# A selective scan: the input increments of every unit's last tile move from VectorE to GpSimd, and that tile's decay from SBUF to PSUM

## The chip, the cores and the metric

The kernel runs on one core of a Trainium2 chip. The metric is the device time of one execution in microseconds (us); lower is better. The engines named below are TensorE (PE in the rows), VectorE (DVE), ScalarE (ACT), GpSimd (POOL) and SyncE (SP), which here only issues DMAs. Each runs its own instruction stream in order, and they wait for each other on semaphores.

## The reference

The program is a convolution-like state-space layer followed by attention and a mixture of experts. The change lies in the first part, a selective scan over images of 4 x 192 channels x 32 x 32, so over L = 1024 positions. There are four directions k: row by row, column by column, and both reversed.

```python
x_dbl = jnp.einsum('bkdl,kcd->bkcl', xs, x_proj_weight)
dts, Bs, Cs = (x_dbl[:, :, :R], x_dbl[:, :, R:R + N], x_dbl[:, :, R + N:])
dt = jax.nn.softplus(dts + bias)
def step(h, inp):
    dtt, ut, bt, ct = inp
    dA = jnp.exp(dtt[..., None] * A)
    h = h * dA + (dtt * ut)[..., None] * bt[:, :, None, :]
    y = jnp.einsum('bkdn,bkn->bkd', h, ct)
    return (h, y)
...
ys = ys + Ds * u;  y = cross_merge(ys);  y = layernorm(y);  out = gelu(y)
```

For each of 192 channels d and 16 states n a first-order recurrence h = h * decay + increment runs over the 1024 positions. The decay is exp(dt * A), the increment is dt * u * B. Each state is then multiplied by C and the 16 are summed.

## The kernel before

**Tiles and units.** A unit is one image b, one direction k and one half f of the channels (96 of them). There are `UNITS = 8` for each image, in the order given by `order(ui)`: p (row order or column order), f, r (forward or reversed). The outer loop `Fori(0, NB, 1)` runs over the four images, so there are 32 units. A unit has `TILES = 12` tiles. A tile holds 32 channels times 4 states on 128 partitions and all 1024 positions: tile t has channel block j = t % 3 and state group nq = t // 3. Each tile is worked in two halves of 512 positions, numbered q = 2t and 2t + 1 in a unit, 24 of them.

**What happens to a half tile q.** TensorE spreads the 4 B rows over the 128 partitions with a selection matrix, into one of the `UR = 4` PSUM banks of `psU` (L426); it waits until scan q - 4 is done, because that one read the bank. VectorE multiplies the bank in place with `dtu_rep`, dt*u replicated to 128 partitions by DMA (L610, called the product below). ScalarE makes the decay of a whole tile in SBUF, `decay` (L519), up to four tiles ahead. VectorE then runs the scan (L655): it reads the decay (SBUF) and the increment (PSUM) and writes `hs`, a ring of 8 tiles in SBUF. The second half of a tile starts from the last state of the first and waits for it.

**After the scan.** GpSimd multiplies the finished tile with the replicated C rows, `c_rep` (L565). TensorE adds up the states of three tiles at a time, one "trip" of 2 x 3 f32 matmuls, into `psY` (L395, `sum_states`). Over two units, forward and reversed, `psY` collects one result. ScalarE copies it to `y_new` (L499, `read_y`, at tile 7 of the next even unit), and GpSimd adds it to `Y` (L547, L550, `add_y`, at tile 6).

**What is prepared for the next unit.** During tiles 0 and 1 of every unit TensorE projects dt of the next one (L359, `z_side`), ScalarE takes it out and makes the softplus, and GpSimd finishes dt after tile 3 (L570) and dt*u after tile 4 (L576). SyncE stores both in DRAM and loads them back replicated (L664), four slots each. In units 2 and 6 TensorE also projects the B and C rows of the next row order or column order at tiles 4 and 5 (L359 again, `row_side`), and GpSimd works on them after tile 8 of that unit and after tile 6 of the next (L582, L591).

**Order of the work.** Nothing is scheduled automatically: each engine's stream is written out in the loops. VectorE issues the product of q + 1 before the scan of q; TensorE issues at position q the spread of q, then the projection, then the trip, if one stands there.

Of the kernel before, what the change touches and what calls it, by code (L numbers as in the profile page):

```python
# [25 lines left out]
NB = 4  # L26
D = 192
HC = 96
# [42 lines left out]
def prepare(nc, w, s):  # L71

    with ExitStack() as ctx:
# [30 lines left out]
        with nc.Block() as block:  # L104
# [36 lines left out]
            def _(pool):  # L141
# [46 lines left out]
                pool.memset(s.X[:, NB, :, :], 0.0)  # L188
# [85 lines left out]
def scan(nc, w, s):  # L274

    with ExitStack() as ctx:
# [6 lines left out]
        HR, DR, UR, RR = 8, 4, 4, 4  # L283
        xt = sb("xt", [HC, 2, L])
# [9 lines left out]
        y_new = sb("y_new", [HC, L])  # L294
# [25 lines left out]
        y_begun = sem("y_begun")  # L320

# [7 lines left out]
        def source(nb, p):  # L329
            return (lambda h, lo, n=CH: xt[:, h, lo:lo + n]) if p else (lambda h, lo, n=CH: s.X[:, nb, h, lo:lo + n])  # L330

        def unit_ahead(b, ui):

            return b + (ui + 1) // UNITS, (ui + 1) % UNITS

        def row_step(b, ui):

            return (b, 1, b * 2 + 1) if ui < 4 else (b + 1, 0, b * 2 + 2)
# [11 lines left out]
        with nc.Block() as block:  # L350
            @block.tensor
            def _(pe):
# [10 lines left out]
                def z_side(q, b, ui):  # L363
# [6 lines left out]
                    if q == 0:  # L370
                        pe.wait_ge(row_taken, b * 4 + (2 if ui < 3 else 4 if ui < 7 else 6))
                        if p:
                            pe.wait_ge(xt_half, nb * 2 + 2)
                    project(psP[0:HC, c, :], s.w_dt[:, k, h, HC * f:HC * f + HC], source(nb, p)(h, CH * c), h, z_proj)

                def row_side(q, b, ui, n):
# [5 lines left out]
                    if q == 8:  # L382
                        pe.wait_ge(z_taken, n * 2 + 4)
                        if p:
                            pe.wait_ge(xt_half, nb * 2 + 2)
# [26 lines left out]
                with pe.Fori(0, NB, 1) as b:  # L412
                    for ui in range(UNITS):
# [29 lines left out]
            def _(act):  # L443
# [48 lines left out]
                def read_y(n, pair, b, ui):  # L492
# [5 lines left out]
                    act.wait_ge(y_added, pair + (1 + START))  # L498
                    nc.scalar.copy(y_new[:], psY[0:HC, :, :].rearrange("p c l -> p (c l)")).then_inc(y_taken, 1)  # L499
# [9 lines left out]
                with act.Fori(0, NB, 1) as b:  # L509
                    for ui in range(UNITS):  # L510
                        n = b * UNITS + ui
                        p, f, r, k = order(ui)
                        for t in range(TILES):
# [4 lines left out]
                            act.wait_ge(scan_done, n * (2 * TILES) + (2 * t + 2 - 2 * DR + S0))  # L518
                            nc.scalar.activation(decay[:, t % DR, :], dt_rep[:, rep_slot(ui, j), :], ACT.Exp,  # L519
# [5 lines left out]
                            if ui == UNITS - 1 and t in (5, 6):  # L525
# [3 lines left out]
                                               s.X[:, b + 1, h, :].rearrange("p (h w) -> p w h", h=HH)  # L529
# [4 lines left out]
            def _(pool):  # L534
                pool.sem_inc(y_added, 1 + START)

# [1385 lines left out]
```

## Time and profile before

| | |
|---|---|
| time, median of 3 runs | 2926.32 us (2926.2 to 2936.25) |
| the profiled execution's own time | 2925.74 us |
| its span | 2923.9 us |
| scan loop, first product to last scan | 66.6 us to 1424.5 us |
| VectorE busy in the whole span | 2180.1 us (75%) |
| GpSimd busy in the whole span | 1266.4 us (43%) |

The scan takes a little under half of the time; attention and the experts follow it and are not touched. How the rows below are read: in a timeline row the first number is the start in us from the span's start, the second how long the group of x instructions took from the first start to the last end, and the square bracket tells how long the engine had sat idle before and what ended that. Neighbouring instructions of one engine overlap a little, so the time that one takes out of the stream is the distance from its start to the next one's start, which is less than its duration.

### The profile page before, as it was taken

The numbers are of one execution on the slowest core, as the hardware profiler recorded it, in microseconds if no ns is written. First come the engines' busy times: TensorE is split into PE (matmuls) and PEld (weight loads), VectorE is DVE, ScalarE is ACT, GpSimd is POOL, SyncE is SP. The second block draws the span as 40 slices with busy tenths as digits, with TensorE's granted clock in tenths as the row PEclk, the third lists the DMA queues.
The fourth block names the chain that finished last, engine by engine and source line by source line (L and its number), as shares of the span: only waits on it lengthen the run. The fifth ranks groups of instructions, "written<-read, shape, count | busy, mean of one in ns | idle before, by whom it ended". The sixth has DMA issues, their size and how long they took to land. (4 is left out here: it accounts for less than half of the span.)

```text
span 2923.9 us, 33177 instructions
## 1 busy us (share of the span) xinstructions
PE 2319.4 (79%) x8931; PEld 816.1 (28%) x8931; DVE 2180.1 (75%) x3002; ACT 1349.9 (46%) x1866; POOL 1266.4 (43%) x651
## 2 busy tenths in 40 slices
PE   3676767667676766667668599999999969999999
PEld 1111111111111111111124122333333227676766
DVE  4999999999999999999656598787878642221212
ACT  3454454445444443544456067676767532222221
POOL 3888887888788788888731200000000020000000
PEclk9777676767777677777669599999999979999999
DMA  4434443443454344345413512131221340000000
GB/s 121 157 118 149 160 135 124 164 158 121 137 162 145 120 156 158 118 139 165 128 34 93 80 16 30 25 45 24 35 33 24 46 126 6 6 6 6 6 6 11
DMA packets 92071, 255.58 MB, mean 87 GB/s; under 512 B 16430, under 2 KB 22129, under 8 KB 91857
## 3 DMA queue, kind: packets, MB, share of 16 engines
q1 hardware_dynamic: 87818, 253.41, 31.1%
q8 instruction: 66, 1.08, 0.2%
q10 hardware_dynamic: 4078, 0.19, 0.1%
q14 instruction: 109, 0.89, 0.1%
HBM read 209.25 MB, written 40.04 MB: 85 GB/s over the span
## 5 line engine op out<-in xcount | busy, mean ns | idle before, releaser
L565 POOL TENSOR_TENSOR hs<-hs,c_rep 128x1024 f32<-128x1024 f32 x384 | 901.0, 2356 | 258.7 <-DVE hs L655 225.1
L426 PE MATMUL psU<-b_stack,b_sel 96*128 96x512 bf16 x768 | 370.4, 492 | 429.9 <-DVE hs L655 428.0
L519 ACT ACTIVATE decay<-dt_rep,a_neg 128x1024 f32<-128x1024 f32 x384 | 437.2, 1145 | 484.1 <-DVE hs L655 470.9
L1529 DVE TENSOR_REDUCE mx<-ps 128x1 f32<-128x512 f32 x864 | 539.3, 682 | 114.7 <-PE ps L1368 109.5
L1504 ACT ACTIVATE P<-ps 128x512 f32<-128x512 f32 x768 | 417.6, 599 | 246.3 <-PE ps L1380 222.0
L610 DVE TENSOR_TENSOR psU<-psU,dtu_rep 128x512 f32<-128x512 f32 x768 | 513.8, 673 | 23.4 <-PE psU L426 13.1
L655 DVE TENSOR_TENSOR_SCAN hs<-decay,hs,psU 128x512 f32<-128x512 f32 x384 | 487.4, 1269 | 1.1
L655 DVE TENSOR_TENSOR_SCAN hs<-decay,psU 128x512 f32<-128x512 f32 x384 | 463.5, 1207 | 0.0
L395 PE MATMUL psY<-hs,state_sel 128*32 128x512 f32 x1572 | 421.4, 895 | 21.5 <-ACT y_new L499 15.4
L1368 PE MATMUL ps<-ks,qs 96*128 96x512 bf16 x864 | 344.2, 403 | 34.6 <-DMA ks<-qk_parts 24.2
L426 PEld LDWEIGHTS psU<-b_stack,b_sel 96*128 96x128 bf16 x768 | 75.9, 100 | 993.0 <-DVE hs L655 869.3
L1817 DVE SCALAR_TENSOR_TENSOR acc<-psE,gate,acc 128x192 f32<-128x192 f32 x128 | 53.5, 418 | 381.9 <-PE psE L1717 378.9
L1380 PE MATMUL ps<-qs,ks 99*128 99x512 bf16 x768 | 293.4, 382 | 0.0
L1755 ACT ACTIVATE hid<-psH,b 128x512 f32<-128x512 f32 x192 | 114.6, 695 | 317.6 <-PE psH L1709 317.6
L1717 PE MATMUL psE<-w,hid 128*128 128x192 f32 x1536 | 257.1, 328 | 0.0
L1717 PEld LDWEIGHTS psE<-w,hid 128*128 128x128 f32 x1536 | 248.8, 190 | 21.2 <-ACT hid L1755 21.2
L1393 PE MATMUL psO<-P,v_now 128*32 128x512 f32 x1536 | 204.5, 605 | 0.0
L1705 PE MATMUL psH<-z_head,w_head 128*128 128x512 f32 x384 | 172.0, 598 | 2.5 <-ACT hid L1755 1.7
L1368 PEld LDWEIGHTS ps<-ks,qs 96*128 96x128 bf16 x864 | 83.8, 98 | 312.9 <-DVE mx L1529 233.6
L1308 POOL COPY v_now<-V 128x1024 f32 (+1 forms) x15 | 15.5, 1038 | 316.9 <-PE psO L1393 316.8
L1300 POOL TENSOR_TENSOR nm<-zero,top 128x32 f32<-128x32 f32 x13 | 3.3, 252 | 344.6 <-DVE top L1533 344.6
L455 ACT ACTIVATE dt<-psP,cols 96x512 f32<-96x512 f32 x66 | 45.1, 683 | 226.3 <-PE psP L359 226.3
(223 smaller groups left out, 2025.8 us busy)
## 6 DMA issues: line engine op xcount, KB each, us to landing
c_rep<-c_rows SPq DMA_DIRECT2D x132, 512.0 KB, 5.2
dt_rep<-dt_rows SPq DMA_DIRECT2D x99, 512.0 KB, 6.4
dtu_rep<-dt_rows SPq DMA_DIRECT2D x99, 512.0 KB, 5.6
dt_rows<-dt SPq DMA_DIRECT2D x33, 384.0 KB, 3.3
dt_rows<-soft SPq DMA_DIRECT2D x33, 384.0 KB, 3.4
qs<-qk_parts SPq DMA_DIRECT2D x90, 128.0 KB, 6.7
ks<-qk_parts SPq DMA_DIRECT2D x90, 128.0 KB, 7.2
qk_parts<-qparts SPq DMA_DIRECT2D x16, 576.0 KB, 3.6
```

What stands on the lines that cost most here:

```text
L395: m = pe.matmul(psY[BLK * j:BLK * j + BLK, c, :], s.state_sel[:], hs[:, h_slot(ui, 3 * trip + j), CH * c:CH * c + CH], start=(trip == (fir ...
L426: pe.matmul(psU[:, q % UR, :], s.b_sel[:, r, nq, :], b_stack[:, p, CH * pos:CH * pos + CH], start=True, stop=True).then_inc(b_spread, 1)
L519: nc.scalar.activation(decay[:, t % DR, :], dt_rep[:, rep_slot(ui, j), :], ACT.Exp, scale=s.a_neg[:, col:col + 1]).then_inc(decay_ready, 1)
L565: pool.tensor_tensor(h, h, c_rep[:, nq, :], ALU.mult).then_inc(hc_ready, 1)
L610: v.tensor_tensor(u, u, dtu_rep[:, rep_slot(ui, j), CH * pos:CH * pos + CH], ALU.mult).then_inc(dbu_ready, 1)
L655: v.tensor_tensor_scan(h, da, du, init, ALU.mult, ALU.add).then_inc(scan_done, 1)
L1368: m = pe.matmul(ps1[:, bank, :], qs[0:KQ, hg, head, 128 * qt:128 * qt + 128], ks[0:KQ, hg, head, CH * c:CH * c + CH], start=True, stop=not ...
L1380: m = pe.matmul(ps2[:, bank, :], ks[0:KM, hg, head, 128 * kt:128 * kt + 128], qs[0:KM, hg, head, CH * qc:CH * qc + CH], start=True, stop=n ...
L1393: m = pe.matmul(psO[32 * head:32 * head + 32, :], v_now[:, kt, GH * hg + head, :], P[:, kt % 2, head, :], start=(kt == 0), stop=(kt == KT ...
L1504: nc.scalar.activation(P[:, kt % 2, head, :], ps2[:, bank, :], ACT.Exp).then_inc(exp_done, 1)
L1529: v.reduce_max(mx[:, slot, u:u + 1], ps1[:, (slot * MAXES + u) % R, :], AX.X).then_inc(max_done, 1)
L1717: m = pe.matmul(psE[:, tt % 2, 0:D], hid[:, e % 2, t, 128 * tt:128 * tt + 128], w2[:, e, t, :], start=(t == 0), stop=(t == HT - 1))
```

## The change

`POOL_TILES = (11,)` names the last tile of each unit. For that tile, and only for it:

- TensorE no longer spreads the B rows, and VectorE no longer makes the two products.
- SyncE loads the 4 B rows that this tile needs, replicated over 128 partitions, into a new tile `b_rep` once per unit. They come from a DRAM buffer that now holds B and C rows (`bc_dram` for `c_dram`).
- GpSimd multiplies `dtu_rep` with `b_rep` into a new tile `du`, four tiles ahead: after its C multiply of tile 7.
- ScalarE writes the decay of this tile into the PSUM banks 2 and 3 of `psU`, which tile 11 no longer needs for increments. It waits for scan 19 of the unit, the last reader of bank 3, where it waited for scan 15 before.
- The scan then reads the decay from PSUM and the increment from SBUF.

Three more things change. The trips of state sums move one tile later on TensorE (`t % 3 == 1` for `t % 3 == 0`). `y_new` shares its memory with `du`, so `read_y` and the increment wait for the `add_y` that came before them. And `X` loses its fifth image, whose memory pays for the new tiles: what is worked ahead behind the last image is now image 0 again.

```diff
-                pool.memset(s.X[:, NB, :, :], 0.0)
...
+        POOL_TILES = (11,)
+        MADE = len(POOL_TILES)
+        AHEAD = 4
+        SPREAD = 2 * (TILES - MADE)
...
-        y_new = sb("y_new", [HC, L])
+        b_rep = sb("b_rep", [128, L])
+        du = sb("du", [128, MADE, L])
+        y_new = du[0:HC, MADE - 1, :]
...
+        def decay_of(t, r):
+
+            if t in POOL_TILES:
+                banks = psU[:, 2 * t % UR:2 * t % UR + 2, :]
+                return banks[:, ::-1, :] if r else banks
+            return decay[:, t % DR, :].rearrange("p (c l) -> p c l", c=2)
...
-                                pe.wait_ge(scan_done, g + (S0 - UR + 1))
-                                pe.matmul(psU[:, q % UR, :], s.b_sel[:, r, nq, :],
-                                          b_stack[:, p, CH * pos:CH * pos + CH],
-                                          start=True, stop=True).then_inc(b_spread, 1)
+                                if t not in POOL_TILES:
+                                    pe.wait_ge(scan_done, g + (S0 - UR + 1))
+                                    pe.matmul(psU[:, q % UR, :], s.b_sel[:, r, nq, :],
+                                              b_stack[:, p, CH * pos:CH * pos + CH],
+                                              start=True, stop=True).then_inc(b_spread, 1)
                                 z_side(q, b, ui)
                                 row_side(q, b, ui, n)
-                                if t % 3 == 0:
-                                    if t >= 6:
+                                if t % 3 == 1:
+                                    if t >= 7:
...
-                    act.wait_ge(y_added, pair + (1 + START))
+                    act.wait_ge(y_added, pair + (2 + START))
...
+                            if t in POOL_TILES:
+                                act.wait_ge(scan_done, n * (2 * TILES) + (2 * t + 2 - UR + S0))
+                            else:
+                                act.wait_ge(scan_done, n * (2 * TILES) + (2 * t + 2 - 2 * DR + S0))
...
+                def increment(n, b, ui, t):
+
+                    j = t % NBLK
+                    if made(t) == 1:
+                        pool.wait_ge(b_in, n * 16 + 16)
+                        pool.sem_inc(du_begun, 1)
+                    if made(t) == MADE and ui % 2 == 0:
+                        pool.wait_ge(y_added, b * (UNITS // 2) + (ui // 2 + 2 + START))
+                        pool.sem_inc(du_begun, 1)
+                    pool.wait_ge(dtu_in[rep_slot(ui, j)], rep_count(b, ui, j))
+                    pool.tensor_tensor(du[:, made(t) - 1, :], dtu_rep[:, rep_slot(ui, j), :], b_rep[:], ALU.mult
+                                       ).then_inc(du_ready, 1)
...
                             pool.tensor_tensor(h, h, c_rep[:, nq, :], ALU.mult).then_inc(hc_ready, 1)
+                            if t + AHEAD in POOL_TILES:
+                                increment(n, b, ui, t + AHEAD)
...
-                            if q + 1 < 2 * TILES:
+                            if q + 1 < 2 * TILES and (q + 1) // 2 not in POOL_TILES:
                                 product(n, ui, q + 1, b)
...
+                            if t in POOL_TILES:
+                                db = du[:, made(t) - 1, cs]
...
                         load_dtu(nu, 2)
+                        sp.wait_ge(du_ready, n * MADE + (MADE + START))
+                        load_b(nu)
                         c_free(3)
                         load_c(nu, 3)
```

The order of the instructions on VectorE at the end of the first unit, before. TENSOR_TENSOR is a product, SCALAR_TENSOR_TENSOR a scan; ISA and REGISTER_ALU rows prepare waits.

```order
L610 TENSOR_TENSOR psU<-psU,dtu_rep 128x512
L642 REGISTER_ALU
L655 SCALAR_TENSOR_TENSOR hs<-decay,psU 128x512
L608 REGISTER_ALU
L610 TENSOR_TENSOR psU<-psU,dtu_rep 128x512
L645 REGISTER_ALU
L655 SCALAR_TENSOR_TENSOR hs<-decay,hs,psU 128x512
L610 TENSOR_TENSOR psU<-psU,dtu_rep 128x512
L640 REGISTER_ALU
L642 REGISTER_ALU
L655 SCALAR_TENSOR_TENSOR hs<-decay,psU 128x512
L645 REGISTER_ALU
```

The same place in the changed program:

```order
L653 TENSOR_TENSOR psU<-psU,dtu_rep 128x512
L685 REGISTER_ALU
L703 SCALAR_TENSOR_TENSOR hs<-decay,psU 128x512
L691 REGISTER_ALU
L703 SCALAR_TENSOR_TENSOR hs<-decay,hs,psU 128x512
L683 REGISTER_ALU
L685 REGISTER_ALU
L689 REGISTER_ALU
L703 SCALAR_TENSOR_TENSOR hs<-psU,du 128x512
L691 REGISTER_ALU
L703 SCALAR_TENSOR_TENSOR hs<-psU,hs,du 128x512
```

Two products are gone between scans 20, 21 and 22, and four scans stand in a row; the last two read `psU` as decay and `du` as increment.

TensorE at the start of the second unit, before: spread (L426), projection of dt (L359), trip of state sums (L395).

```order
L426 MATMUL psU<-b_stack,b_sel 128x512
L359 MATMUL psP<-X,w_dt 96x512
L393 REGISTER_ALU
L395 MATMUL psY<-hs,state_sel 32x512 x3
L425 REGISTER_ALU
L426 MATMUL psU<-b_stack,b_sel 128x512
L359 MATMUL psP<-X,w_dt 96x512
L395 MATMUL psY<-hs,state_sel 32x512 x3
L425 REGISTER_ALU
L426 MATMUL psU<-b_stack,b_sel 128x512
L359 MATMUL psP<-X,w_dt 96x512
```

And in the changed program:

```order
L451 MATMUL psU<-b_stack,b_sel 128x512
L383 MATMUL psP<-X,w_dt 96x512
L450 REGISTER_ALU
L451 MATMUL psU<-b_stack,b_sel 128x512
L383 MATMUL psP<-X,w_dt 96x512
L450 REGISTER_ALU
L451 MATMUL psU<-b_stack,b_sel 128x512
L383 MATMUL psP<-X,w_dt 96x512
L417 REGISTER_ALU
L419 MATMUL psY<-hs,state_sel 32x512 x3
L450 REGISTER_ALU
L451 MATMUL psU<-b_stack,b_sel 128x512
```

The two halves of the trip stood behind the first and the second spread of the unit and now stand behind the third and the fourth.

GpSimd in the second half of the first unit, changed program (L607 is the C multiply, L592 `add_y`, L576 the new increment):

```order
L607 TENSOR_TENSOR hs<-hs,c_rep 128x1024
L582 ISA
L592 ISA
L592 TENSOR_TENSOR Y<-Y,du 96x32x32
L605 REGISTER_ALU
L607 TENSOR_TENSOR hs<-hs,c_rep 128x1024
L573 REGISTER_ALU
L575 ISA
L576 TENSOR_TENSOR du<-dtu_rep,b_rep 128x1024
L605 REGISTER_ALU
L607 TENSOR_TENSOR hs<-hs,c_rep 128x1024
```

One multiply of full tile size is added behind the C multiply of tile 7; nothing on GpSimd goes.

## Rows read from the trace of the kernel before

**Rows 1.** Windows: us; busy (instructions) of PE, PEld, DVE, ACT, POOL; clock; DMA share, GB/s.

```profile
430.00:785.00 355.00, 241.35 (x678) 45.47 (x678) 350.28 (x402) 163.85 (x164) 294.82 (x126) 0.70 0.45 148
```

**Rows 2.** Waits of VectorE inside the scan loop: total us, times, longest.

```profile
DVE psU L610 <- PE psU L426: 13.1, 15, 2.1
```

**Rows 3.** Timeline of VectorE over the end of a unit without a stall.

```profile
229.49 1.21 DVE L655 TENSOR_TENSOR_SCAN hs<-decay,psU 128x512 f32<-128x512 f32 x1
230.61 0.67 DVE L610 TENSOR_TENSOR psU<-psU,dtu_rep 128x512 f32<-128x512 f32 x1
231.20 1.27 DVE L655 TENSOR_TENSOR_SCAN hs<-decay,hs,psU 128x512 f32<-128x512 f32 x1
232.38 0.67 DVE L610 TENSOR_TENSOR psU<-psU,dtu_rep 128x512 f32<-128x512 f32 x1
232.97 1.21 DVE L655 TENSOR_TENSOR_SCAN hs<-decay,psU 128x512 f32<-128x512 f32 x1
234.21 1.28 DVE L655 TENSOR_TENSOR_SCAN hs<-decay,hs,psU 128x512 f32<-128x512 f32 x1
235.40 1.27 DVE L610 TENSOR_TENSOR psU<-psU,dtu_rep 128x512 f32<-128x512 f32 x2
236.58 1.21 DVE L655 TENSOR_TENSOR_SCAN hs<-decay,psU 128x512 f32<-128x512 f32 x1
```

**Rows 4.** The page's fifth part: the C multiply on GpSimd (busy, mean ns, idle before).

```profile
L565 POOL TENSOR_TENSOR hs<-hs,c_rep 128x1024 f32<-128x1024 f32 x384 | 901.0, 2356 | 258.7 <-DVE hs L655 225.1
```

**Rows 5.** Timeline of GpSimd, second half of the last unit 6.

```profile
1372.13 4.67 POOL L565 TENSOR_TENSOR hs<-hs,c_rep 128x1024 f32<-128x1024 f32 x2
1376.88 2.12 POOL L582 TENSOR_TENSOR rows_bc<-rows_bc,b_stack 32x1024 f32<-32x1024 f32 x1
1379.25 6.98 POOL L565 TENSOR_TENSOR hs<-hs,c_rep 128x1024 f32<-128x1024 f32 x3 [0.25 <-POOL rows_bc L582]
```

**Rows 6.** Timeline of GpSimd and VectorE, end of the last unit.

```profile
1413.90 6.97 POOL L565 TENSOR_TENSOR hs<-hs,c_rep 128x1024 f32<-128x1024 f32 x3 [0.53 <-POOL b_stack L591]
...
1423.23 1.28 DVE L655 TENSOR_TENSOR_SCAN hs<-decay,hs,psU 128x512 f32<-128x512 f32 x1
1424.59 2.34 POOL L565 TENSOR_TENSOR hs<-hs,c_rep 128x1024 f32<-128x1024 f32 x1 [0.68 <-DVE hs L655]
```

**Rows 7.** Timeline of ScalarE in the middle of a unit.

```profile
1330.15 1.15 ACT L519 ACTIVATE decay<-dt_rep,a_neg 128x1024 f32<-128x1024 f32 x1 [2.33 <-DVE hs L655]
```

**Rows 8.** Timeline of TensorE at a unit's start; VectorE's stall there last.

```profile
188.03 0.61 PE L426 MATMUL psU<-b_stack,b_sel 96*128 96x512 bf16 x1 [1.10 <-DVE hs L655]
188.44 1.92 PE L359 MATMUL psP<-xt,w_dt 96*96 96x512 f32 x2
190.28 1.93 PE L395 MATMUL psY<-hs,state_sel 128*32 128x512 f32 x6
...
194.38 1.06 PE L395 MATMUL psY<-hs,state_sel 128*32 128x512 f32 x6
195.37 0.39 PE L426 MATMUL psU<-b_stack,b_sel 96*128 96x512 bf16 x1
195.60 1.02 PE L359 MATMUL psP<-xt,w_dt 96*96 96x512 f32 x2
...
195.80 0.70 DVE L610 TENSOR_TENSOR psU<-psU,dtu_rep 128x512 f32<-128x512 f32 x1 [0.72 <-PE psU L426]
```

**Rows 9.** Windows at and behind that unit's start, columns as in Rows 1.

```profile
188.50:193.50 5.00, 5.00 (x12) 0.96 (x10) 4.96 (x7) 0.00 (x0) 4.75 (x4) 0.50 0.46 166
196.00:199.00 3.00, 2.13 (x7) 0.62 (x5) 3.00 (x4) 2.19 (x4) 1.24 (x1) 1.00 0.51 164
```

**Rows 10.** Timeline of TensorE and VectorE, tiles 4 to 6 of the third unit 6.

```profile
1014.17 0.61 PE L426 MATMUL psU<-b_stack,b_sel 96*128 96x512 bf16 x1
1014.71 1.97 PE L359 MATMUL psP<-X,w_bc 96*64 x2
...
1020.77 1.93 PE L395 MATMUL psY<-hs,state_sel 128*32 128x512 f32 x6 [1.12 <-ACT y_new L499]
...
1023.28 0.70 DVE L610 TENSOR_TENSOR psU<-psU,dtu_rep 128x512 f32<-128x512 f32 x1 [1.71 <-PE psU L426]
```

**Rows 11.** The page's sixth part: a replicating load, count, size, us to landing.

```profile
c_rep<-c_rows SPq DMA_DIRECT2D x132, 512.0 KB, 5.2
```

More of the change, by code:

```diff
@@ L329, in source, with held, spread_index, made @@
         def source(nb, p):
-            return (lambda h, lo, n=CH: xt[:, h, lo:lo + n]) if p else (lambda h, lo, n=CH: s.X[:, nb, h, lo:lo + n])
+            return (lambda h, lo, n=CH: xt[:, h, lo:lo + n]) if p else (lambda h, lo, n=CH: s.X[:, held(nb), h, lo:lo + n])
+        def held(nb):
+            return nb if isinstance(nb, int) else nb[0]
         def unit_ahead(b, ui):
-            return b + (ui + 1) // UNITS, (ui + 1) % UNITS
+            return ((b + 1) % NB,) if ui == UNITS - 1 else (b,), (ui + 1) % UNITS
         def row_step(b, ui):
-            return (b, 1, b * 2 + 1) if ui < 4 else (b + 1, 0, b * 2 + 2)
+            return ((b,), 1, b * 2 + 1) if ui < 4 else (((b + 1) % NB,), 0, b * 2 + 2)
+        def spread_index(q):
+            return q - 2 * sum(m < q // 2 for m in POOL_TILES)
+        def made(t):
+            return POOL_TILES.index(t) + 1
         def rep_slot(ui, j):
@@ L497, in read_y @@
                     act.wait_ge(summed, n * SUB + (2 * SUB + 1 + START))
-                    act.wait_ge(y_added, pair + (1 + START))
-                    nc.scalar.copy(y_new[:], psY[0:HC, :, :].rearrange("p c l -> p (c l)")).then_inc(y_taken, 1)
+                    act.wait_ge(y_added, pair + (2 + START))
+                    nc.scalar.copy(y_new, psY[0:HC, :, :].rearrange("p c l -> p (c l)")).then_inc(y_taken, 1)
                 nc.scalar.preload_act_table_set("natural_log_exp_and_others")
@@ L546, in add_y @@
                     if p == 0:
[L547 removed]
+                        pool.tensor_tensor(y, y, y_new, ALU.add).then_inc(y_added, 1)
                     else:
                         yt = y.rearrange("p (h w) -> p w h", h=HH)
[L550 removed]
+                        pool.tensor_tensor(yt, yt, y_new.rearrange("p (w h) -> p w h", w=WW), ALU.add).then_inc(y_added, 1)
                 pool.memset(hs[:], 0.0).then_inc(hc_ready, TILES)
@@ L642, in _ @@
                                 v.wait_ge(decay_ready, n * TILES + (t + 1))
-                            v.wait_ge(dbu_ready, g + 1)
+                            if t not in POOL_TILES:
+                                v.wait_ge(dbu_ready, n * SPREAD + (spread_index(q) + 1))
+                            elif q % 2 == 0:
+                                v.wait_ge(du_ready, n * MADE + (made(t) + START))
                             if q % 2:
@@ L673, in load_c, with load_b @@
                     p, f, r, k = order(ui)
-                    src = s.c_dram[p].rearrange("(r q n) l -> r n q l", r=2, q=4)[r, nq]
+                    src = s.bc_dram[p, 1].rearrange("(r q n) l -> r n q l", r=2, q=4)[r, nq]
                     sp.dma_start(c_rep[:, nq, :], src.unsqueeze(0).broadcast_to([BLK, 4, L])).then_inc(c_in[nq], 16)
+                def load_b(ui):
+                    p, f, r, k = order(ui)
+                    src = s.bc_dram[p, 0].rearrange("(r q n) l -> r n q l", r=2, q=4)[r, SUB - 1]
+                    sp.dma_start(b_rep[:], src.unsqueeze(0).broadcast_to([BLK, 4, L])).then_inc(b_in, 16)
                 def store_c(p):
-                    sp.dma_start(s.c_dram[p], rows[C_ROWS, :]).then_inc(c_stored, 16)
+                    sp.dma_start(s.bc_dram[p].rearrange("i n l -> (i n) l"), rows[0:4 * N, :]).then_inc(c_stored, 16)
                 sp.wait_ge(row_taken, 2)
@@ L703, in c_free, with rep_free @@
                             sp.wait_ge(hc_ready, n * TILES + (3 * nq + 3 + TILES + START))
+                        def rep_free(t, now):
+                            if t in POOL_TILES:
+                                sp.wait_ge(du_ready, n * MADE + (made(t) - MADE * (1 - now) + START))
+                            elif now:
+                                sp.wait_ge(dbu_ready, n * SPREAD + (spread_index(2 * t + 1) + 1))
+                            else:
+                                sp.wait_ge(dbu_ready, n * SPREAD + 2)
                         sp.wait_ge(dt_ready, n + 2)
```

36 lines of the change are left out of this document (18 added, 18 removed).

## The prediction

> **What bounds the kernel now.** I read the waits of the scan loop first, then the busy times of a stretch in its middle, then the timeline of each engine around a unit's end. Over 355 us in the middle of the loop VectorE is busy for 350.28, or 98.7%; GpSimd is next with 294.82, 83% [rows 1]. VectorE waits for TensorE only 13.1 us in all, in 15 places [rows 2]. The reader should see that the loop is one VectorE stream, scan behind product behind scan [rows 3], so that anything taken out of it is gained, and anything given to GpSimd is free only while its 17% lasts. The loop lasts from 66.6 to 1424.5 us; what follows isn't touched, and I leave it at its time.
>
> **VectorE.** Durations overlap, so I count from start to start. From scan 20 of a unit to the first product of the next: 235.40 - 229.49 = 5.91 us [rows 3]. It is made of scan 20 (1.12), a product (0.59), scan 21 (1.18), a product (0.59), scan 22 (1.24, since scan 23 waits for its end) and scan 23 (1.19). Afterwards four scans stand in a row. Scan 21 waits for scan 20 as 23 does for 22, so scan 20 takes 1.24. A scan that follows an independent scan is in no row; its bounds are 1.12 (before a product) and 1.24 (before a dependent scan), and I take 1.19, what scan 23 takes before the next unit's product. Sum 1.24 + 1.19 + 1.24 + 1.19 = 4.86, so 1.05 us less per unit, 33.6 us over 32 units (32 to 36 by the bounds). That the last two scans read the decay from PSUM and the increment from SBUF I cost at nothing: they read one PSUM and one SBUF operand before and after. The largest difference between two forms of the scan in the rows is 1.28 against 1.21 [rows 3], which on 64 scans would be 4.5 us either way.
>
> The Trainium skill (VectorE: DVE Perf Modes, "The TRN2 errata — SBUF-src ops pay a fixed extra latency per instruction") gives an instruction that reads PSUM 120 cycles beside its 512 elements, at 0.96 GHz, an estimate of 0.66 us; the trace's duration of 0.67 agrees. By that price 64 products would be 42 us instead of the 37.8 that 0.59 from start to start gives.
>
> **GpSimd.** It gets 32 multiplies of 128 x 1024. Nearest row: the C multiply, 2.36 us long [rows 4], 2.33 from start to start (6.98 for three) [rows 5]; the new one is 2.33, 75 us in all. In a usual unit it falls into the slack of 3.48 - 2.33 = 1.15 us per tile, 3.48 being VectorE's time for a tile (two products of 0.59, scans of 1.12 and 1.18). The fullest unit is 6, with `add_y` and the row work. There the C multiply of tile 7 starts at 1372.13, so the increment runs from 1374.46 to 1376.8 [rows 5]. Scan 22, which needs it, starts 2.43 before the next unit; that unit now starts 1.05 earlier than 1382.54, at 1381.49, so at 1379.06: 2.3 us to spare, the thinnest margin. The rest of that unit's GpSimd work ends 2.33 later, at 1388.6, 7.1 behind the unit's end where 3.7 was usual. The next unit's first multiply, wanted 4.24 behind its start, comes 2.8 late; at 1.15 per tile this is gone after three tiles, before dt is due at tile 3. Its readers in between are the state sums, which now stand a tile later.
>
> At the very end nothing makes up for the delay. Before, the last multiply starts at 1424.59, when the last scan is done [rows 6]. Afterwards tiles 7, 8, the increment, 9, 10 and 11 follow without a gap: 1413.90 + 5 x 2.33 = 1425.55 on the same start of the unit. So the last unit ends 0.96 us later instead of 1.05 earlier: 2.0 us of the 33.6 go back, and 31.6 stay.
>
> **ScalarE.** The decay of tile 11 can now start only when scan 19 is done. Scan 22 starts 0.59 + 1.24 + 1.19 = 3.0 later. The decay takes 1.15, and ScalarE is idle 2.33 before each one [rows 7], so about 1.8 is to spare; the decays of tiles 0 and 1 queue behind it and are needed 4 and 7 us later. No row shows such a write to PSUM; between 1.15 less and 1.8 more nothing follows from it.
>
> **Copies and loads.** One load of 512 KB per unit, like those of C that land in 5.2 us [rows 11]. SyncE's wait before it is met long before (the increment is four tiles old), it stands behind all `dtu_rep` loads, and it has 36 us until its reader. DMA share 0.45 [rows 1] becomes about 0.49. Cost 0; if it pushed a `dtu_rep` load, that one still has some 5 us. The memset of X that goes lies ahead of a barrier at which GpSimd then waits; 0.
>
> **TensorE, where the choice is.** At a unit's start it works without a gap: spread, projection, trip, at 1.2 GHz (granted 0.50), and then at 2.4 GHz (1.00) [rows 8, 9]. At 1.2 the steps are 0.41, 1.84 and 1.86 apart, at 2.4 some 0.23, 0.95 and 0.99. Going through the 31 unit starts in this view, I find the rise between 0.9 before and 1.7 behind the first product, and where it is last, VectorE waits 0.7 for spread 2 [rows 8]. These waits sum to 6.3 of the 13.1; 4.1 belong to the ends of the image loop and stay; 2.7 come where TensorE waits for `y_new` at tile 6 of units 2 and 6 [rows 10], and go, as the trip is a tile later. With the new order the group starts at -3.6 (scan 20 done) instead of -4.65, so I set the rise at 0.1 to 2.7. Spread 2 is then at 0.9, in time for product 2 at 2.3. With the latest rise the projection ends at 2.9, the trip at 3.9, product 3 starts at 4.3 where 4.07 was wanted, and product 4 at 6.5 instead of 6.03: 0.7 again; with a rise before 1.4 nothing. So these 6.3 stay about as they are. New is that in units 2 and 6 the trip falls on the projection of the rows, positions 8 and 9: at 1.2 GHz 0.54 + 1.90 [rows 10] + 1.86 = 4.3 for each, against 1.75 of VectorE. Starting slow and rising midway costs about 0.4, at 2.4 GHz nothing, all at 1.2 GHz 2.3 + 0.7 + 0.7 = 3.7. Eight such units: 0 to 30, I take 3, since the rows there were mostly at the higher level before (7 of 8 units). -2.7 + 3 is nothing.
>
> **Sum.** 2925.7 of the profiled execution (0.6 under the median of the runs) - 33.6 + 2.0 = 2894.1; against the median 2894.7. I say 2894.5.
>
> **The rivals.**
> - *TensorE takes part of it back* at the row projections. For it: the third unit 6 stayed at 1.2 GHz from tile 4 to tile 6 and cost VectorE 2.3 us even in the easier order [rows 10]. Against: one of eight. All eight slow: 2894.5 + 27 = 2921; half of them, 2908.
> - *TensorE stalls go away*: if the clock is already up when the later trip comes, up to 9 us less than forecast, 2886.
> - *The price of a whole product*: VectorE's full 0.67 for each, another 5 us, 2889; against it, the overlap in every pair of [rows 3]. The page named above leads to the same time.
> - *Slower*: the clock doesn't rise before the moved trip is over. Then at every unit's start spread 3 comes at 5.0 and product 3 at 5.65 (1.6 late), spread 4 at 9.1 and product 4 2.4 late: 4.0 us per unit against 1.05 gained and 0.2 that it cost before. 31 x 3.8 - 31.6 = 86 more than before, 3012. It decides once the rise comes later than about 4 us behind the first product. Against: the latest seen is 1.7.
> - *It doesn't do what it says*: the increment or the decay comes late for scan 22, or the mixed scans are slower. It needs 1.05 us per unit to cancel, 0.26 per tail scan or the 1.8 to 2.3 us of margin used up and 1.05 more; 2926.
>
> The Trainium skill (SBUF — State Buffer, "Who interferes with whom") says that a VectorE instruction with two SBUF inputs shuts GpSimd out and is shut out by it for a whole instruction. The scan with an initial value from `hs` beside an SBUF decay shows none of that (1.27 to 1.28 while GpSimd is 83% busy), so such a value doesn't count. Had the decay of tile 11 stayed in SBUF beside `du`, 64 scans could by the rule each wait up to 2.33 us, 149 in all; written to PSUM it can't come to that.
>
> **How the numbers follow.** Forecast 0.61 (its own range 2889 to 2903), TensorE takes part back 0.17, stalls gone 0.08, whole price 0.05, slower 0.05, doesn't do it 0.04. About 0.5% is what a measurement of this kernel can tell from no change: 14.6 us, so faster means under 2911.7. That holds for the forecast, for the two cases below it and for a bit over half of the case that TensorE takes part back: 0.61 + 0.08 + 0.05 + 0.10 = 0.84. Same 0.11, slower 0.05. The range leaves out little below and some 0.13 above: 2885 to 2912.
>
> **What would show it.** Right: 704 products, from scan 20 to the next unit's product 4.8 to 4.9 us, units of 40.8 instead of 41.9, the last C multiply about 1 to 2 us behind the last scan, no wait of VectorE for `du` or a decay. Wrong: a sum of VectorE's waits for TensorE well above 13, at tile 5 of units 2 and 6 or at spreads 3 and 4; scans of the tail longer than 1.28; or GpSimd's lag at a unit's start that doesn't go away by tile 3.

## The result and the profile after

The changed kernel takes 2906.5 us (median of 5 runs, 2902.7 to 2911.3) against 2926.4 for the kernel before (median of 5, 2926.2 to 2936.3). The ratio is 0.9924, 95% interval 0.9905 to 0.9943: 0.8% faster. The forecast was 2894.5, a gain of 31.6; some 20 us of it came. The profiled execution took 2904.9 us (span 2903.0), 20.9 less than the one of before.

First the windows view over the same 355 us as [rows 1], the same columns:

```profile
430.00:785.00 355.00, 239.76 (x682) 46.94 (x681) 346.04 (x390) 165.22 (x170) 316.95 (x136) 0.72 0.48 162
```

GpSimd went from 294.82 to 316.95 us, VectorE from 350.28 to 346.04: it waits more than before. The timeline of VectorE at a unit's end without a stall answers to [rows 3]. With it stand the first products of two units that follow one another:

```profile
191.22 1.27 DVE L653 TENSOR_TENSOR psU<-psU,dtu_rep 128x512 f32<-128x512 f32 x2
...
227.18 1.22 DVE L703 TENSOR_TENSOR_SCAN hs<-decay,psU 128x512 f32<-128x512 f32 x1
228.44 1.28 DVE L703 TENSOR_TENSOR_SCAN hs<-decay,hs,psU 128x512 f32<-128x512 f32 x1
229.63 1.20 DVE L703 TENSOR_TENSOR_SCAN hs<-psU,du 128x512 f32<-128x512 f32 x1
230.87 1.28 DVE L703 TENSOR_TENSOR_SCAN hs<-psU,hs,du 128x512 f32<-128x512 f32 x1
232.07 1.27 DVE L653 TENSOR_TENSOR psU<-psU,dtu_rep 128x512 f32<-128x512 f32 x2
```

From start to start the four scans take 1.26, 1.19, 1.24 and 1.20, and the unit 232.07 - 191.22 = 40.85 instead of 41.88. The groups with the shapes apart (busy, mean ns, idle before) show what the new operations cost:

```profile
L703 DVE TENSOR_TENSOR_SCAN hs<-psU,hs,du 128x512 f32<-128x512 f32 x32 | 41.1, 1283 | 1.1
L703 DVE TENSOR_TENSOR_SCAN hs<-psU,du 128x512 f32<-128x512 f32 x32 | 38.3, 1198 | 0.0
L576 POOL TENSOR_TENSOR du<-dtu_rep,b_rep 128x1024 f32<-128x1024 f32 x32 | 75.2, 2351 | 0.0
L547 ACT ACTIVATE psU<-dt_rep,a_neg 128x1024 f32<-128x1024 f32 x32 | 35.8, 1118 | 297.2 <-DVE hs L703 297.2
```

The scans are no slower, the increment takes what a C multiply takes (2.35 us), and none of the scans waits for an operand (1.1 us idle in all). So the gain of a unit is there 32 times. The waits of VectorE's products (total us, times, longest) show what is given back; [rows 2] is the view before:

```profile
DVE psU L653 <- issue: 14.6, 3, 5.3
DVE psU L653 <- PE psU L451: 9.2, 16, 1.3
DVE psU L653 <- DMA dtu_rep<-dt_rows: 7.1, 2, 6.2
```

The three waits in the first line are the three turns of the image loop, where VectorE jumps back to the loop's start; `issue` stands for time in which it waited for nothing that the profile shows. Here is one of them, VectorE and then SyncE's issues, before and after. Before:

```profile
402.52 1.28 DVE L655 TENSOR_TENSOR_SCAN hs<-decay,hs,psU 128x512 f32<-128x512 f32 x1
405.89 1.30 DVE L610 TENSOR_TENSOR psU<-psU,dtu_rep 128x512 f32<-128x512 f32 x2 [2.09 <-PE psU L426]
...
397.87 0.51 SPq L675 DMA_DIRECT2D c_rep<-c_rows  x1
398.49 0.54 SPq L664 DMA_DIRECT2D dtu_rep<-dt_rows  x1
```

After:

```profile
394.88 1.28 DVE L703 TENSOR_TENSOR_SCAN hs<-psU,hs,du 128x512 f32<-128x512 f32 x1
401.20 1.30 DVE L653 TENSOR_TENSOR psU<-psU,dtu_rep 128x512 f32<-128x512 f32 x2 [5.04 <-issue]
...
393.28 0.51 SPq L723 DMA_DIRECT2D c_rep<-bc_rows  x1
393.90 0.54 SPq L712 DMA_DIRECT2D dtu_rep<-dt_rows  x1
394.49 0.59 SPq L728 DMA_DIRECT2D b_rep<-bc_rows  x1
```

Before, the last two loads of a turn were issued 5.9 and 5.3 us ahead of the end of scan 23. Now there are three, 2.9, 2.3 and 1.7 ahead. The idle time grew from 2.09, 1.82 and 2.03 (5.9) to 5.04, 4.32 and 5.29 (14.7). The name of TensorE in the bracket of before doesn't explain it: the spread that this product needs had ended at 399.68, 6 us earlier; in the changed kernel, where the bracket says `issue`, at 392.86, 8 us earlier. The DMA queues (packets, MB, share of the 16 engines) show more. After, from 396.2 to 399.0 and from 399 to 400:

```profile
q1 hardware_dynamic: 224, 0.81, 80.3%
...
q1 hardware_dynamic: 74, 0.25, 67.8%
q14 instruction: 2, 0.02, 3.9%
```

Before, from 403.4 to 403.8, the end of its scan 23, and in the 0.8 us behind that:

```profile
q14 instruction: 1, 0.01, 8.9%
...
DMA packets 0, 0.00 MB, mean 0 GB/s; under 512 B 0, under 2 KB 0, under 8 KB 0
```

In the first stretch no packet of the queue that the profile calls `instruction` moves, and the loads fill the queues; the instruction packets come at 399.10 and 399.91, and VectorE starts at 401.20. Before, the loads were all but done, an instruction packet went out at 403.64, and VectorE started at 405.89. The traces show this distance everywhere: at each of the 36 turns of the twelve profiled executions of this document, an instruction packet starts 1.99 to 2.25 us ahead of VectorE's first product, whether the idle time was 0.1 or 5.3 us. So what varies is when that packet goes out.

Where the 20.9 us came from, in the two profiled executions:

| part | change, us |
|---|---|
| until the first product (66.59, now 64.79) | -1.8 |
| 32 units, 1.04 each | -33.3 |
| three turns of the image loop (5.9, now 14.7) | +8.7 |
| other waits of VectorE for TensorE (9.0, now 9.2) | +0.2 |
| a wait for `dtu_rep` at the start | +0.9 |
| last scan to the end of the last C multiply (2.42, now 3.99) | +1.6 |
| all that follows, from the first instruction that reads `Y` on VectorE (1485.6, now 1488.1) | +2.5 |

The parts add up to -21.2, which leaves 0.3 without a place. The last part is not touched, and in twelve profiled executions it took between 1483.3 and 1491.7. It and the first part are scatter.

At the end of the last unit, which answers to [rows 6], GpSimd runs without a gap, and its last multiply starts 1.65 us behind the end of the last scan, at 1401.10, where 2.1 was worked out:

```profile
1391.86 2.35 POOL L576 TENSOR_TENSOR du<-dtu_rep,b_rep 128x1024 f32<-128x1024 f32 x1
1394.17 9.26 POOL L607 TENSOR_TENSOR hs<-hs,c_rep 128x1024 f32<-128x1024 f32 x4
...
1398.16 1.28 DVE L703 TENSOR_TENSOR_SCAN hs<-psU,hs,du 128x512 f32<-128x512 f32 x1
```

### The profile page after: what moved, and what is told of

The parts are those of the page before. It is cut to its first block and busy times, and to the rows that moved or that the text cites. A ratio compares the mean times of both kernels' runs of the same rounds, so it can differ in the third digit from the quotient of the medians.

```text
span 2903.0 us, 33227 instructions
## 1 busy us (share of the span) xinstructions
PE 2299.2 (79%) x8867; PEld 817.2 (28%) x8867; DVE 2146.0 (74%) x2938; ACT 1341.8 (46%) x1866; POOL 1334.3 (46%) x682
## 3 DMA queue, kind: packets, MB, share of 16 engines
q8 instruction: 64, 1.05, 0.2%
## 5 line engine op out<-in xcount | busy, mean ns | idle before, releaser
L607 POOL TENSOR_TENSOR hs<-hs,c_rep 128x1024 f32<-128x1024 f32 x384 | 899.0, 2354 | 165.0 <-DVE hs L703 131.8
L451 PE MATMUL psU<-b_stack,b_sel 96*128 96x512 bf16 x704 | 337.1, 492 | 442.8 <-DVE hs L703 441.1
L547 ACT ACTIVATE decay<-dt_rep,a_neg 128x1024 f32<-128x1024 f32 x352 | 396.7, 1142 | 256.2 <-DVE hs L703 240.7
L653 DVE TENSOR_TENSOR psU<-psU,dtu_rep 128x512 f32<-128x512 f32 x704 | 476.1, 681 | 31.2 <-issue 14.6
L703 DVE TENSOR_TENSOR_SCAN hs<-decay,hs,psU 128x512 f32<-128x512 f32 x352 | 449.4, 1277 | 1.1
L703 DVE TENSOR_TENSOR_SCAN hs<-decay,psU 128x512 f32<-128x512 f32 x352 | 427.9, 1216 | 0.0
L419 PE MATMUL psY<-hs,state_sel 128*32 128x512 f32 x1572 | 410.9, 874 | 11.6 <-POOL hs L607 7.5
L451 PEld LDWEIGHTS psU<-b_stack,b_sel 96*128 96x128 bf16 x704 | 68.7, 102 | 965.1 <-DVE hs L703 872.8
L1783 PEld LDWEIGHTS psE<-w,hid 128*128 128x128 f32 x1536 | 248.8, 190 | 21.2 <-ACT hid L1821 21.2
L547 ACT ACTIVATE psU<-dt_rep,a_neg 128x1024 f32<-128x1024 f32 x32 | 35.8, 1118 | 297.2 <-DVE hs L703 297.2
```

What stands on the lines that cost most here:

```text
L419: m = pe.matmul(psY[BLK * j:BLK * j + BLK, c, :], s.state_sel[:], hs[:, h_slot(ui, 3 * trip + j), CH * c:CH * c + CH], start=(trip == (fir ...
L451: pe.matmul(psU[:, q % UR, :], s.b_sel[:, r, nq, :], b_stack[:, p, CH * pos:CH * pos + CH], start=True, stop=True).then_inc(b_spread, 1)
L547: nc.scalar.activation(decay_of(t, r), dt_rep[:, rep_slot(ui, j), :].rearrange("p (c l) -> p c l", c=2), ACT.Exp, scale=s.a_neg[:, col:col ...
L607: pool.tensor_tensor(h, h, c_rep[:, nq, :], ALU.mult).then_inc(hc_ready, 1)
L653: v.tensor_tensor(u, u, dtu_rep[:, rep_slot(ui, j), CH * pos:CH * pos + CH], ALU.mult).then_inc(dbu_ready, 1)
L703: v.tensor_tensor_scan(h, da, db, init, ALU.mult, ALU.add).then_inc(scan_done, 1)
```

## The experiments

My theory (T1 where an expectation numbers it) was that the replicating loads which stand close to the loop's turn hold up its restart, because GpSimd's multiply of tile 8 frees their C slot 3 us later and because `b_rep` came on top. The rivals: that the turn got longer by itself, wherever the loads stand (T2 in the expectations), that the moved trips of TensorE cost it, that the new load costs wherever it stands, or that it is scatter.

**The load of B last.** From the changed kernel, in SyncE's order:

```diff
-                        sp.wait_ge(du_ready, n * MADE + (MADE + START))
-                        load_b(nu)
                         c_free(3)
                         load_c(nu, 3)
+                        sp.wait_ge(du_ready, n * MADE + (MADE + START))
+                        load_b(nu)
```

> The changed kernel, with the load of b_rep issued behind the last load of c_rep instead of before it, so that it starts some 6 us later, behind the turn of the image loop. Theory T1: at each of the three turns VectorE must fetch its next instructions, and the fetch waits in the DMA engines behind the replicating loads in flight (dtu_rep, b_rep). Then the idle time there falls from 5.0 to 5.3 us to between 2 and 4 (the dtu_rep load still stands there), and the time to 2899 to 2903. Rival T2: the turn got longer because VectorE's stream in the loop has more rows (1614 against 1574) or because of a wait at its top; then the place of a load changes nothing: idle 5 us, time 2906.

Measured: 2898.4 us, ratio 0.9889 (0.9868 to 0.9910). The turns were idle for 4.47, 4.39 and 4.25, 13.1 in all, against 14.7. One of them, VectorE and SyncE:

```profile
398.93 1.30 DVE L653 TENSOR_TENSOR psU<-psU,dtu_rep 128x512 f32<-128x512 f32 x2 [4.47 <-issue]
...
391.58 0.51 SPq L723 DMA_DIRECT2D c_rep<-bc_rows  x1
392.21 0.57 SPq L712 DMA_DIRECT2D dtu_rep<-dt_rows  x1
```

So `b_rep` itself makes only 1.6 us of the 8.7, and the turns stayed above the 2 to 4 that I had expected. The two loads that before also had are enough once they are late.

**`dtu_rep` ahead of `c_rep` too.** From the kernel of the first experiment:

```diff
-                        c_free(2)
-                        load_c(nu, 2)
                         rep_free(10, 1)
                         load_dtu(nu, 2)
+                        c_free(2)
+                        load_c(nu, 2)
```

> As the last one, and the load of dtu_rep for tile 2 of the next unit is issued as soon as its product is done, ahead of the wait for GpSimd's multiply of tile 8 and the load of c_rep behind it. T1: now no load but c_rep is in flight at the turn; idle 2 us as before the change, time 2896 to 2900. T2: idle 5 us, time 2906.

Measured: 2896.8 us, ratio 0.9890 (0.987 to 0.991). Turns 2.45, 2.15 and 2.38, 7.0 in all; the waits for TensorE 6.4 in 14 places:

```profile
397.12 1.30 DVE L653 TENSOR_TENSOR psU<-psU,dtu_rep 128x512 f32<-128x512 f32 x2 [2.45 <-issue]
...
389.83 0.51 SPq L712 DMA_DIRECT2D dtu_rep<-dt_rows  x1
391.79 7.46 SPq L723 DMA_DIRECT2D c_rep<-bc_rows  x2
```

One 512 KB load is issued in the last 4 us instead of three, and the idle is nearly that of before: the order of SyncE's issues alone gives the turns back. Against the changed kernel the ratio is 0.0034 lower, 10 us, about what the turns (7.7) and TensorE (2.8) add up to, though the two intervals just overlap. Against the first experiment the two profiled executions differ by 10.1 us, the medians by 1.6 only; that experiment's runs go from 2890.4 to 2906.3, its profiled one being the longest, so the medians can't tell the two apart.

**The same, with the load of B left early.**

```diff
-                        c_free(2)
-                        load_c(nu, 2)
                         rep_free(10, 1)
                         load_dtu(nu, 2)
+                        c_free(2)
+                        load_c(nu, 2)
                         sp.wait_ge(du_ready, n * MADE + (MADE + START))
                         load_b(nu)
```

> The changed kernel with only the second half of the second experiment: dtu_rep for tile 2 is loaded ahead of the wait for GpSimd and of c_rep; b_rep stays in its old place, which is now right behind c_rep. If it is the number of loads in flight at the turn that counts, dtu_rep is gone from there, but c_rep and b_rep together still are: idle 3 to 4.5 us, time 2899 to 2903. If it is dtu_rep alone that VectorE waits for there, idle 2.2 and 2897.

Measured: 2898.0 us, ratio 0.9909 (0.9894 to 0.9924), turns 3.62, 4.92 and 3.66, 12.2 in all. With `c_rep` and `b_rep` still close to the turn, `dtu_rep` first saves little at the turns; `b_rep` has to go as well. The time is 8 us under that of the next kernel, run on the same chip, more than the 1.8 of the turns and the 1.0 of TensorE (7.6 against 8.6) that I can point to.

**The changed kernel once more.**

> The changed kernel itself once more, on the same chip as the last: idle 5 us at each turn, ratio to the kernel before 0.992 to 0.993.

Measured: 2906.2 us, ratio 0.9930 (0.9916 to 0.9943); turns 4.83, 4.35 and 4.85, 14.0 in all. The idle time at the turns comes back each time.

**The kernel before with a load of its own size more.** Into the kernel before, at the place of the load of B, a replicating load of 512 KB that nobody reads:

```diff
+                def load_spare(ui):
+                    ...
+                    sp.dma_start(spare.rearrange("(a q) l -> a q l", q=4), src.unsqueeze(0).broadcast_to([BLK, 4, L])).then_inc(spare_in, 16)
                         load_dtu(nu, 2)
+                        load_spare(nu)
                         c_free(3)
```

> The kernel before, with one more replicating DMA of 512 KB per unit at the place where the changed kernel loads b_rep (rows of C, written to DRAM memory that nobody reads). T1: the idle time of VectorE at the three turns grows from 2.0 to 3 to 5 us and the time by 3 to 9, to 2929 to 2935, with all units elsewhere unchanged at 41.9. T2: turns stay at 2.0 and the time at 2926.

Measured: 2926.2 us, ratio 0.9989 (0.9977 to 1.0001): no change. One turn grew, 3.42, the others (2.35, 2.03) hardly:

```profile
402.17 1.28 DVE L657 TENSOR_TENSOR_SCAN hs<-decay,hs,psU 128x512 f32<-128x512 f32 x1
406.87 1.30 DVE L612 TENSOR_TENSOR psU<-psU,dtu_rep 128x512 f32<-128x512 f32 x2 [3.42 <-PE psU L428]
...
398.76 0.56 SPq L683 DMA_DIRECT2D spare<-c_rows  x1
```

This was a miss for the size that I expected. The load was issued 4.7 us ahead of the end of scan 23, where the changed kernel issues it 1.7 ahead; it took 5.8 to 7.2 us and landed 2.5, 1.1 and 2.0 behind the scan, against 5.6, 4.7 and 6.1 in the changed kernel. That fits a cost that depends on when an extra load comes, not on its being there. Away from the turns one unit took 47.1 us instead of 41.9; TensorE waited 2.2 us for `y_new` in it.

**No increment on GpSimd.** From the first experiment's kernel. GpSimd makes 16 of the 1024 columns, and the scans of the last tile read `b_rep` in its place, so the increment of that tile is left out:

```diff
-                    pool.tensor_tensor(du[:, made(t) - 1, :], dtu_rep[:, rep_slot(ui, j), :], b_rep[:], ALU.mult
+                    pool.tensor_tensor(du[:, made(t) - 1, 0:16], dtu_rep[:, rep_slot(ui, j), 0:16], b_rep[:, 0:16], ALU.mult
...
-                                db = du[:, made(t) - 1, cs]
+                                db = b_rep[:, cs]
```

> As the first experiment (b_rep loaded late), but GpSimd makes only 16 of the 1024 columns of each increment, and the scans of tile 11 read b_rep in place of du: the work that the change put on GpSimd is left out, everything else stays. If GpSimd's 75 us were hidden but for their lag, then the lag goes: the load of dtu_rep for tile 2 comes some 3 us earlier against the end of a unit, VectorE's idle time at the three turns of the image loop falls from 4.4 to 2 to 3 us, the last C multiply starts with the end of the last scan (2 us less), and the time is 2898 - 6 - 2 = 2890. If it were more than hidden, units too would be shorter than 40.84.

Measured: 2886.1 us, ratio 0.9855 (0.9836 to 0.9873). The turns are back at 2.06, 1.96 and 1.96, with SyncE's order unchanged, and the units at 40.84:

```profile
396.18 1.30 DVE L653 TENSOR_TENSOR psU<-psU,dtu_rep 128x512 f32<-128x512 f32 x2 [2.06 <-issue]
```

That closes the link: GpSimd's 2.35 us don't touch a unit, but they hold back the loads that wait for its multiplies (here the last two are issued 5.0 and 4.4 us ahead of the end of scan 23, against 2.9 and 2.3), and these reach the turn. In all they cost some 12 us of the first experiment's 2898.4: 7.1 at the turns, 3.3 of waits for TensorE, the rest at the end of the loop.

**The trips a tile later, alone.** In the kernel before:

```diff
-                                if t % 3 == 0:
-                                    if t >= 6:
+                                if t % 3 == 1:
+                                    if t >= 7:
```

> The kernel before, with only the trips of state sums moved one tile later on TensorE. The prediction's sum has this part at nothing: 6.3 us of stalls at unit starts stay, 2.7 at tile 6 of units 2 and 6 go, about 3 come at tiles 4 and 5 there: 2926, within 3. Its rival, that TensorE takes part of the gain back at the row projections, says 8 us or more on top, 2934, with VectorE waiting for spreads 10 to 12 of units 2 and 6.

Measured: 2931.4 us, ratio 1.0010 (0.9999 to 1.0021). The waits for TensorE are 14.3 and those at the turns 5.7, together 20.0 against 14.9:

```profile
DVE psU L610 <- PE psU L426: 14.3, 22, 2.3
DVE psU L610 <- issue: 5.7, 3, 2.0
```

Without the shorter tail the move costs up to 5 us by these waits; by the ratio the time is the same. Of the parts in the prediction, 3.6 came at tiles 4 and 5 of units 2 and 6, where 3 were taken, but the 6.3 at unit starts, which it let stay, became 10.7.

**The trips back at their old tile.** In the kernel of the second experiment, the same edit the other way round.

> As the second experiment, with the trips of state sums back at their old place on TensorE (behind spreads 0 and 1 of every third tile). Moving them in the kernel before cost nothing that could be told (ratio 1.001) but raised VectorE's waits for TensorE from 15 to 20 us. If that holds here, this kernel is 2 to 5 us faster than the second experiment, 2892 to 2895. Rival: with the start of a unit nearer to TensorE's first matmuls by 1 us the old order is the worse one, waits above 10 us, 2900.

Measured: 2919.3 us, ratio 0.9967 (0.9952 to 0.9981), 22 us above the second experiment. VectorE's waits for TensorE are 29.1 in 48 places, against 6.4 in 14. I had expected a few us less, and even my rival said 2900, so this was a plain miss. TensorE and VectorE at a unit's start:

```profile
229.38 0.61 PE L451 MATMUL psU<-b_stack,b_sel 96*128 96x512 bf16 x1 [4.80 <-DVE hs L703]
...
231.62 1.93 PE L419 MATMUL psY<-hs,state_sel 128*32 128x512 f32 x6
233.48 0.61 PE L451 MATMUL psU<-b_stack,b_sel 96*128 96x512 bf16 x1
...
232.98 0.67 DVE L653 TENSOR_TENSOR psU<-psU,dtu_rep 128x512 f32<-128x512 f32 x1
234.13 0.70 DVE L653 TENSOR_TENSOR psU<-psU,dtu_rep 128x512 f32<-128x512 f32 x1 [0.47 <-PE psU L451]
237.24 0.70 DVE L653 TENSOR_TENSOR psU<-psU,dtu_rep 128x512 f32<-128x512 f32 x1 [1.29 <-PE psU L451]
```

In this order, as in the kernel before, the first half trip stands ahead of spread 1. But spread 0 can start only when scan 20 is done, and with two products fewer behind that scan the next unit's first product now comes 3.60 us behind spread 0 (232.98 - 229.38), where it was 4.66 before (192.69 - 188.03). Spread 1 starts at 233.48 and is late for product 1. With the shorter tail the later trip is no side matter: without it two thirds of the second experiment's gain are gone (10.6 of 33.2 us stay).

**The tail's decay in SBUF.** In the kernel of the second experiment the decay of tile 11 stays in SBUF beside `du`:

```diff
-            if t in POOL_TILES:
-                banks = psU[:, 2 * t % UR:2 * t % UR + 2, :]
-                return banks[:, ::-1, :] if r else banks
```

> As the second experiment, but the decay of tile 11 stays in SBUF, so that the 64 scans of this tile have two SBUF inputs and no PSUM operand. By the rule that such an instruction and one of GpSimd shut each other out, each such scan waits for the multiply under way, 1.2 to 2.3 us: 75 to 150 more, 2970 to 3045, with scan or idle rows to show it. Rival: no contention, 2896, scans of 1.2 to 1.28 us.

Measured: 2987.4 us, ratio 1.0199 (1.0178 to 1.0219), 90 us above the second experiment. Its two kinds of tail scans (shortest/median/longest ns), and one such scan beside GpSimd:

```profile
L698 DVE TENSOR_TENSOR_SCAN hs<-decay,du x32: 1198/2936/5682, 103.1 to 1478.2; 128x512 f32<-128x512 f32 x32
L698 DVE TENSOR_TENSOR_SCAN hs<-decay,hs,du x32: 1283/3184/3205, 108.8 to 1481.2; 128x512 f32<-128x512 f32 x32
...
194.81 3.19 DVE L698 TENSOR_TENSOR_SCAN hs<-decay,hs,du 128x512 f32<-128x512 f32 x1
193.95 6.21 POOL L602 TENSOR_TENSOR hs<-hs,c_rep 128x1024 f32<-128x1024 f32 x2 [0.25 <-POOL rows_bc L621]
```

Of the 64 tail scans 16 are as long as in the changed kernel, 1.20 to 1.28; eight of these ran while no GpSimd instruction did, the other eight had started 0.16 ahead of a multiply, which then took 3.2. 40 took 2.7 to 3.2, and eight took 5.1 to 5.7: each of these had two multiplies beside it, one behind the other, and ended 1.1 behind the second. Together the 64 took 185.7 us, against 79.4 in the second experiment. 32 of GpSimd's C multiplies grew as well, to 3.0 to 3.3 us (2 in 6.21 instead of 4.66 above). Units took 42.75 to 45.7. The PSUM copy is what makes the change a gain at all. At the three turns VectorE was idle for 0.30, 0.20 and 0.14 only: the last scan took 3.2 us, and the instruction packet went out 1.7 to 1.8 ahead of its end, where it was 0.2 ahead before.

**Two tiles on GpSimd.** In the kernel of the second experiment, `POOL_TILES = (10, 11)`, and a wait on `du_ready` ahead of GpSimd's work on the C rows.

> The changed kernel with the loads of the second experiment (dtu_rep first, b_rep last), and tiles 10 and 11 of each unit made by GpSimd, both with their decay in PSUM, so 1280 scans of which 128 read mixed operands, and 640 products. If VectorE stays the bound, a unit takes 40.84 - 1.1 = 39.75 us and the time falls by another 30 to 35, to about 2864. Rival: GpSimd has 28.0 + 4.7 + 4.7 + 1.3 + 1.1 = 39.8 us of work in a mean unit and 42.6 in a unit 6, so it becomes the bound there, VectorE waits for du or for free tiles of hs, and the time is 2875 to 2890.

Measured: 2890.4 us, ratio 0.9865 (0.9845 to 0.9886), the rival's case at its upper edge and the fastest of the complete kernels, though its interval overlaps the second experiment's. GpSimd becomes the bound in part of the units: VectorE waits for `du`, where before it never did. The waits, and one of them with GpSimd's stream before it:

```profile
DVE hs L705 <- POOL du L576: 25.1, 21, 2.2
DVE psU L655 <- PE psU L451: 8.6, 10, 1.2
...
228.40 4.66 POOL L607 TENSOR_TENSOR hs<-hs,c_rep 128x1024 f32<-128x1024 f32 x2
228.47 1.22 DVE L705 TENSOR_TENSOR_SCAN hs<-psU,du 128x512 f32<-128x512 f32 x1 [2.19 <-POOL du L576]
```

Another 33 us of products were taken out, and all but 6 came back: 25.1 as waits for `du`.

## Why the prediction came out as it did

The sign and the mechanism of the gain held, and 2906.5 lies in the range of 2885 to 2912. But it lies outside the 2889 to 2903 of the forecast's own case, and no rival names what took the missing 12 us; the range had been widened for a TensorE that takes part back, which didn't happen. So that the range covers it is in part luck. By its own steps:

- **VectorE, 1.05 us per unit:** right, 1.04. The tail takes 4.89 from start to start where 4.86 was worked out. The trace also refutes the rival with a product's whole price, by which a unit would have lost another 0.16.
- **The mixed scans at nothing:** right, 1198 and 1283 ns against 1.2 and 1.28.
- **ScalarE:** right; the write to PSUM takes 1118 ns, the one to SBUF 1142, and no scan waits for it.
- **GpSimd, inside the units:** right: 2351 ns, no wait for `du`, a lag that goes away. At the end of the loop 1.6 us go back (3.99 - 2.42), where 2.0 were worked out.
- **The ends of the image loop, "4.1 ... stay", and "Copies and loads. ... Cost 0":** this step failed, and it holds 8.7 of the 10.7 us between the gain worked out (31.6) and that of the profiled execution (20.9). I followed GpSimd's 2.3 us of lag to the scans and to the last multiply, but not to SyncE, which waits in `c_free(2)` for the multiply of tile 8 and has `dtu_rep` and now `b_rep` queued behind it. I also took the idle at the turn for something that no load bears on. GpSimd's multiply of tile 8 ended 6.0 us ahead of the unit's end before and ends 2.9 ahead now. None of the signs that the prediction lists as wrong looks at the turns. The runs show the cause from three sides: reorder the loads (turns of 7.0), take GpSimd's work away (6.0), or leave it (14.7 and 14.0).
- **TensorE, "-2.7 + 3 is nothing":** the sum is right (+0.2), its parts roughly. The waits for `y_new` at tile 6 went. At tiles 4 and 5 of units 2 and 6 there are 0.38, 0.37, 0.84 and 0.85, 2.4 in all, where I took 3. What I had not seen is how much rests on the later trip: 22 us.

One unit start of the changed kernel still shows what remains of the stalls that the prediction calls about as they are, here TensorE and then VectorE:

```profile
109.60 1.93 PE L419 MATMUL psY<-hs,state_sel 128*32 128x512 f32 x6
112.11 0.70 DVE L653 TENSOR_TENSOR psU<-psU,dtu_rep 128x512 f32<-128x512 f32 x1 [1.25 <-PE psU L451]
```

And the windows view over that start, columns as in [rows 1]:

```profile
108.50:111.50 3.00, 3.00 (x9) 0.24 (x8) 2.36 (x3) 1.50 (x2) 3.00 (x3) 0.50 0.70 283
```

Granted 0.50, so 1.2 GHz, the half trip takes 1.86, and the product behind it is 1.25 late. That is more than the 0.7 of the prediction, but it is rare: 16 waits make 9.2 us. The slower rival needed it at every unit.

**The rule on two SBUF inputs.** With decay and `du` in SBUF most tail scans took 2.7 to 3.2 us instead of 1.2 to 1.3. The Trainium skill (SBUF — State Buffer, "Who interferes with whom") says that such an instruction and GpSimd's shut each other out; the trace agrees, GpSimd's multiplies grow in the same places. The prediction's 149 us held for the sum (the scans grew by 106 us, the kernel by 90), but not for the single scan: it allowed each a wait of one multiply, 2.33 us, and eight scans waited for two and took 3.9 to 4.5 longer.

**What stays open.** That the loads delay the instruction packets, and these the restart, is read from the order of events in the queues. The runs show that the idle follows the loads, and the constant 2 us from packet to product at 36 turns speaks for the second half; none moved the packets alone. In the kernel before with one load more, the same 512 KB with 4.7 us to spare cost 1.3 in one turn and 0.5 or nothing in the others, so how far a load has to be from the turn is not settled. The first experiment and the one with `dtu_rep` alone first are 10 and 8 us faster than the changed kernel by their ratios or medians, while their turns explain 1.6 and 1.8. Since the untouched part alone differs by up to 8 us from one profiled execution to another, I can't place the rest.

## What to carry to other kernels

When an engine gets more work, follow its delay through every semaphore that it signals, to the DMA issuer as well: a buffer that comes free 3 us later moves a load, and everything queued behind it. Look where a burst of loads lands relative to a loop's turn; issue what is free early ahead of what has to wait, as the second experiment does: its two moves together take 7.7 us off the turns, either one alone 1.6 to 1.8. And when a stage gets shorter, check what else stands in its order: the later trip, which looks like a detail of the diff, decides over more than half of the gain.

## What the runs showed of the hardware

At all 36 turns of the outer loop VectorE's first instruction came 1.99 to 2.25 us behind the start of an instruction packet. The idle time that this left at a turn:

| run | 512 KB loads issued in the last 7.5 us ahead of the last scan's end | idle, us |
|---|---|---|
| before; trips later | 5.9 and 5.3 us ahead | 1.8 to 2.1 |
| before with one load more | 5.9, 5.3 and 4.7 | 2.0 to 3.4 |
| no increment | 5.0 and 4.4 | 2.0 to 2.1 |
| second experiment; trips back | 4.8 and 2.9 | 2.1 to 2.6 |
| `dtu_rep` first alone | 4.8, 2.9 and 2.3 | 3.6 to 4.9 |
| `b_rep` late | 2.9 and 2.3 | 4.3 to 4.5 |
| changed kernel, both times | 2.9, 2.3 and 1.7 | 4.3 to 5.3 |
| two tiles on GpSimd | 7.0 and 0.2 | 1.8 to 1.9 |
| decay in SBUF, last scan 3.2 us long | 6.6 | 0.1 to 0.3 |

In the run with a load issued 0.2 us ahead, an instruction packet started within 0.2 us of the scan's end, and the load's own packets came 1.1 to 1.3 behind it.

Two f32 operands in SBUF, beside a GpSimd that is mostly busy, cost a scan of 512 columns 1.7 to 1.9 us by the median, up to 4.5 where it waited for two multiplies, and nothing where GpSimd was idle or started later. An initial value from SBUF cost 0.06 to 0.09.
